# One chain of full-sized steps in the balancing loop in place of two half-sized chains in turns

## The reference

```python
def sinkhorn_log(logits, num_iters=50, tau=0.1):
    Z = logits / tau
    ...
    def step(carry, _):
        u, v = carry
        u = -jax.nn.logsumexp(Z + v[..., None, :], axis=-1)
        v = -jax.nn.logsumexp(Z + u[..., :, None], axis=-2)
        return ((u, v), None)
    (u, v), _ = jax.lax.scan(step, (u0, v0), None, length=num_iters)
    return jnp.exp(Z + u[..., :, None] + v[..., None, :])
...
H_res = sinkhorn_log(H_res_logits)
...
H_res = (1.0 - g) * I + g * H_res
...
x_mixed = jnp.einsum('btij,btjc->btic', H_res, x_streams)
```

## Time and profile before

| | us |
|---|---|
| median of 3 runs | 1589.5 |
| lowest and highest of them | 1584.46, 1593.9 |
| the profiled execution, its own time | 1587.23 |
| span of its trace, first to last instruction | 1585.5 |
| VectorE busy in it | 829.8 (52%) |
| TensorE matmuls busy in it | 1080.2 (68%) |
| mean granted TensorE clock | 0.847 |

### The profile page before, as it was taken

The page is one execution under the profiler, slowest core; times in us unless marked ns, Lnnn a source line. Parts: engine busy times, 40 slices in busy tenths (PEclk is TensorE's granted clock), DMA queues, the critical chain, the costliest instruction groups (busy, mean ns, idle before and its releaser), DMA issues. The chain is left out here.

```text
span 1585.5 us, 21544 instructions
## 1 busy us (share of the span) xinstructions
PE 1080.2 (68%) x7522; PEld 466.3 (29%) x7522; DVE 829.8 (52%) x1718; ACT 561.1 (35%) x736; POOL 337.0 (21%) x439
## 2 busy tenths in 40 slices
PE   3789877999897747740011567777873980889777
PEld 2333333444343432330001211111241440333343
DVE  4387732222112433279976397777137461877334
ACT  2156661333200304340042236666614000466602
POOL 2323321454300401100055200000002671133200
PEclk9779997999999879965555859999985995799998
DMA  3500002112001250020000411000003134421001
GB/s 107 147 14 22 12 1 80 60 60 80 1 0 44 63 120 1 1 75 0 0 1 0 142 32 30 17 16 1 1 0 116 33 115 113 68 42 22 1 0 53
DMA packets 50147, 67.05 MB, mean 42 GB/s; under 512 B 6077, under 2 KB 40369, under 8 KB 50061
## 3 DMA queue, kind: packets, MB, share of 16 engines
q1 hardware_dynamic: 47816, 60.77, 14.2%
q0 software_dynamic: 2256, 5.26, 1.1%
HBM read 46.93 MB, written 18.82 MB: 41 GB/s over the span
## 5 line engine op out<-in xcount | busy, mean ns | idle before, releaser
L667 DVE TENSOR_REDUCE a2a_mx<-a2a_ring 128x2 f32<-128x1024 f32 x128 | 150.9, 1219 | 47.5 <-PE a2a_ring L535 47.0
L75 PE MATMUL f_pp<-xt,f_wgu 128*128 128x512 f16 x672 | 150.0, 384 | 3.5 <-POOL f_wgu L1102 3.5
L623 ACT ACTIVATE a2a_pr<-a2a_ring 128x1024 f32<-128x1024 f32 x128 | 129.5, 1024 | 61.3 <-PE a2a_ring L567 61.0
L667 DVE TENSOR_REDUCE a3a_mx<-a3a_ring 128x2 f32<-128x768 f32 (+3 forms) x88 | 96.2, 1123 | 33.0 <-PE a3a_ring L535 31.7
L667 DVE TENSOR_REDUCE a0a_mx<-a0a_ring 128x2 f32<-128x768 f32 (+3 forms) x88 | 96.1, 1122 | 29.8 <-PE a0a_ring L535 28.4
L175 POOL TENSOR_TENSOR p_w<-s_w,p_w 128x544 f16<-128x544 f32 (+2 forms) x6 | 15.2, 2549 | 452.9 <-ACT p_w L197 452.9
L623 ACT ACTIVATE a0a_pr<-a0a_ring 128x1024 f32<-128x1024 f32 x80 | 81.0, 1023 | 42.4 <-PE a0a_ring L567 42.0
L623 ACT ACTIVATE a3a_pr<-a3a_ring 128x1024 f32<-128x1024 f32 x80 | 81.1, 1023 | 42.3 <-PE a3a_ring L567 42.0
L75 PEld LDWEIGHTS f_pp<-xt,f_wgu 128*128 128x128 f16 x672 | 65.4, 99 | 85.5 <-issue 6.8
L183 PE MATMUL n_pt<-ident,s_xn 128*128 128x128 f32 x96 | 17.7, 369 | 100.6 <-DVE s_xn L158 100.6
L1076 DVE TENSOR_TENSOR f_sd<-f_sd,f_pp 128x512 f32<-128x512 f32 x28 | 19.2, 687 | 122.3 <-ACT f_sd L1091 122.3
(11 more groups left out here) (278 smaller groups left out, 2030.5 us busy)
## 6 DMA issues: line engine op xcount, KB each, us to landing
stack_scratch<-p_qk SPq DMA_DIRECT2D x126, 128.0 KB
f_ws<-in_L_gu SPq DMA_DIRECT2D x14, 512.0 KB
f_ws<-in_L_down SPq DMA_DIRECT2D x14, 256.0 KB
a0a_qs<-stack_scratch SPq DMA_DIRECT2D x16, 192.0 KB, 3.5
a2a_qs<-stack_scratch SPq DMA_DIRECT2D x16, 192.0 KB, 3.8
s_w<-in_L_w SPq DMA_DIRECT2D x4, 768.0 KB, 5.8
a3a_qs<-stack_scratch SPq DMA_DIRECT2D x16, 192.0 KB, 5.0
a3a_ks<-stack_scratch SPq DMA_DIRECT2D x16, 192.0 KB, 5.3
```

The costliest lines, as they stand in the source:

```text
L75: mm = pe.matmul(out, left(a, c), right(b, c), start=first and k == 0, stop=last and k == n - 1)
L623: act.activation(pr[:, og % 2, u, :, 0:width], ring[:, f % 3, :, 0:width], ACT.Exp, scale=a.scale).then_inc(exped, 1)
L667: dve.tensor_reduce(mx[:, n % 2, i, :, p0:p0 + heads], ring[:, k.max_fill[m] % 3, :, 0:heads * keys].rearrange("q h (p k) -> q h p k", k=k ...
```

## The change

In each pass the six steps are now written once, for all eight tiles: twice as many elements in an instruction, six instructions in place of twelve. Each step is followed by a wait for its own count, the last one as well, so that a wait stands at the end of the pass, ahead of the loop's register add and branch, and none ahead of the first step of a pass. The initial `sem_inc` and the wait behind the loop are gone. The arithmetic, its order for a token and the number of passes are the same.

```diff
-                dve.sem_inc(balanced, 2)
+                byrow = mix[:, :, :].rearrange("p t (i j) -> p (t i) j", j=n)
+                bycol = mix[:, :, :].rearrange("p t (i j) -> p t j i", j=n)
                 with dve.Fori(0, iters) as it:
-                    for k in range(6):
-                        for half in range(2):
-                            tiles = slice(half * NI, (half + 1) * NI)
-                            own = slice(half * NI * n, (half + 1) * NI * n)
-
-                            dve.wait_ge(balanced, it * 12 + (2 * k + half + 1))
-                            byrow = mix[:, tiles, :].rearrange("p t (i j) -> p (t i) j", j=n)
-                            bycol = mix[:, tiles, :].rearrange("p t (i j) -> p t j i", j=n)
-                            sums, inverse = m4[:, own], i4[:, own]
-                            if k == 0:
-                                op = dve.tensor_reduce(sums, byrow, AX.X, ALU.add)
...
-                            op.then_inc(balanced, 1)
-                dve.wait_ge(balanced, 12 * iters + 2)
+                    dve.tensor_reduce(m4[:, :], byrow, AX.X, ALU.add).then_inc(balanced, 1)
+                    dve.wait_ge(balanced, it * 6 + 1)
+                    dve.reciprocal(i4[:, :], m4[:, :]).then_inc(balanced, 1)
+                    dve.wait_ge(balanced, it * 6 + 2)
+                    dve.tensor_tensor(byrow, byrow, i4[:, :].unsqueeze(2).to_broadcast([P, NT * n, n]),
+                                      ALU.mult).then_inc(balanced, 1)
+                    dve.wait_ge(balanced, it * 6 + 3)
+                    dve.tensor_reduce(m4[:, :].rearrange("p (t j) -> p t j", j=n), bycol, AX.X, ALU.add).then_inc(balanced, 1)
+                    dve.wait_ge(balanced, it * 6 + 4)
+                    dve.reciprocal(i4[:, :], m4[:, :]).then_inc(balanced, 1)
+                    dve.wait_ge(balanced, it * 6 + 5)
+                    dve.tensor_tensor(bycol, bycol, i4[:, :].rearrange("p (t j) -> p t j", j=n).unsqueeze(3)
+                                      .to_broadcast([P, NT, n, n]), ALU.mult).then_inc(balanced, 1)
+                    dve.wait_ge(balanced, it * 6 + 6)
                 binary.scales(dve)
```

## The result

The changed kernel takes 1618.93 us (median of 4 runs, 1614.88 to 1620.49) against 1587.24 for the kernel before beside it (4 runs, 1584.46 to 1593.9): a ratio of 1.0189, with a 95% interval from 1.0149 to 1.023. In a later set (5 runs beside 11 of the kernel before) it took 1620.71 against 1587.26, a ratio of 1.0215 (1.0195 to 1.0235). By the two ratios it is slower by 30 and 34 us, with intervals that reach from 24 to 37; 31.5 were forecast.

The account below looks back on a forecast made before the run. VectorE's balancing loop was taken to bound the kernel: 1.994 us durations + 0.225 gaps + 0.35 edge = 2.57 us a pass, 128.5 us against 97.0, so 1589.5 + 31.5 = 1621 us, range 1605 to 1631.

Parts of the forecast that it names:

- The loop is on the path whole: VectorE's balancing loop: nothing else is late, so what it takes longer or shorter, the program does.
- The six durations: The full-width arithmetic instructions of one pass, nothing hiding them: 1994 ns together, range 1892 to 2008.
- The row steps: Row reduction and row multiply of a pass, 128 elements each: 288 and 291 ns.
- The reciprocals: Two a pass, 32 elements each, scaled from smaller sizes: 340 ns each, range 327 to 345.
- The column steps: Column reduction and multiply, reading with a step of four elements, extra growing by element: 360 and 375 ns.
- The gaps: Five waits between the steps inside a pass, 45 ns each: 225 ns, range 150 to 250.
- The edge: From a pass's last multiply to the next reduction, register add and branch in the open: 0.35 us, range 0.08 to 0.40.
- The sum: One pass of the loop 2.57 us, 50 passes 128.5 us against 97.0: plus 31.5 us.
- The pitch rival: Dependent full-sized steps in the loop follow at instruction pitch: 1.60 us a pass, 17 us less, 1572.5 us; chance 0.03.
- The rival of the page: Loop's instructions each have a fixed part of 156 ns; 300 fewer bring about 47 us, 1542.7 us; no separate chance.
- The cheap edge: Loop's branch partly covered, column extra fixed: 2.12 to 2.42 us a pass, 9 to 24 us more; chance 0.10.
- the dear edge: Sequencer needs 0.6 us from last multiply to next reduction: 2.82 us a pass, 44 us more, 1633.5 us; chance 0.04.

Follow-up runs that it names:

- the halves: The kernel before, each step issued for two halves of the tiles in turns: 1587.24 us, loop 97.0 us.
- the halves apart: Half-sized steps in the changed kernel's form of loop, all 50 passes of one half, then of the other: 1693.19 us, one run, loop 203.3 us.
- The wait at the head: Changed kernel with the wait for the column multiply moved from the body's end to before the next pass's first reduction: ratio 1.0134, loop 112.5 us.
- the quarters: Kernel before with four quarters of the tiles in turns in place of two, five passes a body: 1628.29 us, one run, loop 134.3 us.
- the halves in the same body: Kernel before with five passes in one body of the loop: 1581.64 us, ratio 0.9973, loop 92.3 us.
- Written out: Kernel before with all 50 passes written out, no loop and constant waits: 1580.98 us, ratio 0.9958, loop 89.4 us.

## Why the prediction was right, point by point

- **The loop is on the path whole.** Right: every loop that was lengthened or shortened, from 85.2 to 203.3 us, moved the profiled span by as much, within the 7 us by which the rest scatters.
- **The six durations.** 1994 ns forecast, 2044 measured. The row steps were right to 2 ns. The reciprocals were mis-sized by 13 ns each (340 against 353): between 16 and 32 elements it is 6.25 ns an element (253 to 353), more than either of the two scalings, so that 353 lies above even the high end of 345. The column steps were 378 and 382 against 360 and 375. By elements and not fixed was the right choice, but both lie above their high ends, 364 and 375, and the halves in the overlapped loop (253 against 215) had an extra of 38 ns where alone they have 41 (261 against 220). So the measured sum of 2044 lies above the range given for it, 1892 to 2008. What the "SBUF — State Buffer" page of the Trainium skill says in its note on cachelines, that every access to a new 16-byte line pays, agrees in direction with what this trace shows: 92 ns on 128 elements, 0.7 ns each; no figure stands there to compare.
- **The gaps.** 0.225 forecast, 0.17 measured, 0.034 each. The 45 ns from the loop of halves belong to two halves in turns: half-sized steps with nothing between them have 0.03 to 0.04 as well (the timeline of the halves apart). The 0.03 of the chain ahead of the loop was the better row.
- **The edge.** 0.35 forecast, 0.38 measured. The sum of wait and 0.33, 0.37, was nearer than the 0.35 after the subtraction for a count that is no longer worked out. The wait at the head shows that the add and the branch cost nothing beside a last step of 0.38; beside the halves' last step of 0.26 they still cost 0.15.
- **The sum.** 2.57 us a pass and 128.5 in all, measured 2.60 and 129.9. The misses of the three terms, +0.05, -0.05 and +0.03, nearly cancel. The path, the lost overlap and the open edge were right as a mechanism; that the sum came within 1.4 us is in part luck, for the low durations were offset by a high gap.
- **The pitch rival** is excluded: no dependent step starts before 0.03 after the end of the one that it needs. Instructions that do not wait for each other do have a pitch (0.149 in the halves, 0.112 in the quarters), but the full-sized steps here never come to it.
- **The rival of the page.** "VectorE: DVE Perf Modes" of the Trainium skill advises, for chained operations, to minimize their count and not the semaphores; half the count was 32.9 us slower here, and 15.5 with the wait at the head of the pass. A part of each instruction that does not depend on its width is there, 154 ns by the rows above, but it was not there to be saved, since the halves already hid much of it behind each other. In the other direction the advice holds: twice the count, the quarters, was 42 us slower than the halves in the same body (134.3 against 92.3).
- **The cheap edge and the dear edge** are excluded by the 0.38 and by the 378 and 382 ns.

## What to carry to other kernels

When a chain of small dependent steps sets the time, count for each step its duration and the gap, and look for a second independent chain before making the steps wider: one half alone would need an estimated 1.69 us a pass (the durations and gaps of the halves apart, without the open edge), and two in turns need 1.78, so the second half costs 0.09 us. Four chains already cost more instructions than they hide. Keep a wait out of the end of a loop's body; at the head of the next pass it lets the add and the branch run beside the last step, which was worth 0.35 us a pass here, where that step lasts 0.38. And take the price of a wider step from a row of that width where there is one, above all for reciprocals and for operands that are read with a step.

## What the runs showed of the hardware that I had not expected

- An fp32 operand written with a step of four elements lengthens the instruction as one that is read so does (260 against 217 ns at 64 elements, 385 against 292 at 128), but the next independent instruction starts 0.13 after it all the same, where a read with a step holds it back to 0.16 or 0.17.
- The edge of a body five times as long leaves 0.60 us from the first column multiply to the next reduction, against 0.49 in the short body, though the work between is the same. Written out, 600 instructions ran at the same inner pace of 1.78 us a pass as in a loop, so fetching them cost nothing that shows.
- A reciprocal of 32 elements takes 353 ns, one of 16 takes 253: 6.25 ns an element, about six times what a contiguous multiply pays (292 ns for 128 elements against 224 for 64 with the halves apart, 1.1 ns each).
